# Two transformer layers on one core: ACT writes the rounded high parts from PSUM, and Pool splits the row minima

## The reference, cut to what matters

```
tgt1 = layer_norm(tgt, g1, be1)
score = einsum(q, k) / sqrt(HD) + (1 - mask) * -1e9      # q, k, v from tgt1
tgt = tgt + softmax(score) @ v @ Wo.T + bo
tgt = tgt + (memory @ Wg.T + bg)
tgt1 = layer_norm(tgt, g2, be2)
return tgt + relu(tgt1 @ W1.T + b1) @ W2.T + b2
```

## Time and profile before

| | |
|---|---|
| time, median of 3 runs | 1756.74 us (1756.67 to 1759.3) |
| profiled execution: its time | 1759.88 us |
| profiled execution: its span, first to last instruction | 1757.8 us |
| busy: PE, DVE, ACT, POOL | 1485.4, 1438.7, 939.3, 730.6 us |
| mean granted clock of PE | 0.939 |
| instructions | 42638 |

### The profile page before, as it was taken

The page is one execution under the profiler, slowest core; times in us unless marked ns, Lnnn a source line. Parts: engine busy times, 40 slices in busy tenths (PEclk is TensorE's granted clock), DMA queues, the critical chain, the costliest instruction groups (busy, mean ns, idle before and its releaser), DMA issues.

```text
span 1757.8 us, 42638 instructions
## 1 busy us (share of the span) xinstructions
PE 1485.4 (85%) x13376; PEld 1203.8 (68%) x13376; DVE 1438.7 (82%) x4560; ACT 939.3 (53%) x1849; POOL 730.6 (42%) x612
## 2 busy tenths in 40 slices
PE   2789999999999999677777777778889898998987
PEld 1568787888878887555655555556777776777756
DVE  2889888898988997787888788888888888888762
ACT  2666666666666654344444545454555545555451
POOL 3345444454544555423232222334444444444423
PEclk8799999999999999888898988899999999999998
DMA  5555445445544445454546464756444554445400
GB/s 139 135 120 130 106 96 114 103 108 118 116 114 96 121 96 129 104 120 96 120 103 116 100 117 107 138 114 118 99 95 92 113 112 92 93 100 112 88 25 12
DMA packets 163509, 185.73 MB, mean 106 GB/s; under 512 B 15952, under 2 KB 140240, under 8 KB 163408
## 3 DMA queue, kind: packets, MB, share of 16 engines
q1 hardware_dynamic: 163408, 184.57, 48.3%
HBM read 125.78 MB, written 58.72 MB: 105 GB/s over the span
## 4 chain that ended last, share of the span: by engine, by line
PE 55%; DVE 24%; issue 11%; POOL 3%; ACT 2%; DMA 2%; DVEq 1%; SPq 1%; ACTq 0%
PE d_ps L436 25%; PE d_ps L672 7%; PE o_ps L571 6%; DVE prob L849 6%; PE s_ps L493 6%; PE t_ps L507 4%; PE t_ps L541 4%; DVE top_rest L862 2%; PE m_ps L443 2%; POOL k_f L1062 2%; DMA k_stack<-parts 1%; DVE prob_t L1022 1%; DVE stats L871 1%; DVE o_q L911 1%; DVE k_part L934 1%
## 5 line engine op out<-in xcount | busy, mean ns | idle before, releaser
L720 ACT ACTIVATE prob_t<-t_ps 128x384 f32<-128x384 f32 (+1 forms) x512 | 275.7, 545 | 416.2 <-PE t_ps L541 212.6
L493 PE MATMUL s_ps<-k_stack,q_stack 96*128 96x256 bf16 (+1 forms) x1536 | 298.1, 277 | 102.5 <-DVE top L849 42.4
L711 ACT ACTIVATE prob<-prob,neg_max 128x256 f32<-128x256 f32 x512 | 233.0, 505 | 194.7 <-DVE neg_max L849 192.0
L493 PEld LDWEIGHTS s_ps<-k_stack,q_stack 96*128 96x128 bf16 x1536 | 116.2, 101 | 211.7 <-DVE top L849 66.0
L541 PE MATMUL t_ps<-q_stack,k_stack 108*128 108x256 bf16 (+1 forms) x1024 | 214.2, 276 | 8.7 <-ACT q_stack L728 8.6
L1062 POOL TENSOR_TENSOR h_lo<-h_f,h_hi 128x512 fp32r<-128x512 f32 x128 | 167.6, 1309 | 128.6 <-DVE h_hi L949 128.6
L849 DVE CUSTOM_DVE_ANT_0 prob<-s_ps,bias_sb 128x256 f32<-128x256 f32 x512 | 192.9, 416 | 22.0 <-PE s_ps L493 13.7
L571 PE MATMUL o_ps<-prob_t,v_sb 128*17 128x256 f32 (+1 forms) x3072 | 197.7, 377 | 0.0
L834 DVE TENSOR_REDUCE top<-s_ps 128x2 f32<-128x512 f32 x256 | 171.3, 680 | 23.0 <-PE s_ps L493 23.0
L728 ACT ACTIVATE q_stack<-o_ps 12x1024 bf16<-12x1024 f32 x128 | 130.2, 1017 | 106.7 <-PE o_ps L520 105.0
L849 DVE CUSTOM_DVE_ANT_0 prob<-s_ps,causal 128x128 f32<-128x128 f32 (+1 forms) x512 | 156.9, 349 | 34.6 <-PE s_ps L493 33.7
(11 more groups left out here) (113 smaller groups left out, 4148.3 us busy)
## 6 DMA issues: line engine op xcount, KB each, us to landing
q_stack<-parts SPq DMA_DIRECT2D x288, 128.0 KB, 4.1
k_stack<-parts SPq DMA_DIRECT2D x288, 128.0 KB, 6.4
parts<-q_part SPq DMA_DIRECT2D x96, 192.0 KB, 2.3
parts<-k_part SPq DMA_DIRECT2D x96, 192.0 KB, 2.3
ct_kept<-ct_hl SPq DMA_DIRECT2D x16, 512.0 KB, 7.7
x_in<-x_mid SPq DMA_DIRECT2D x32, 256.0 KB, 2.8
x_res<-x_mid SPq DMA_DIRECT2D x32, 256.0 KB, 2.9
ct_hl<-ct_kept SPq DMA_DIRECT2D x16, 512.0 KB, 8.0
```

Source lines behind the costliest of these rows:

```text
L493: last = mm(s_ps[:, h % 2, q * S:q * S + n], q_stack[0:ROWS, t.par, HEAD[h], q * P:(q + 1) * P], k_stack[0:ROWS, t.par, HEAD[h], 0:n], sta ...
L711: last = nc.scalar.activation(prob[:, h % 4, q, :], prob[:, h % 4, q, :], ACT.Exp, bias=neg_max[:, h % 4, q:q + 1], scale=-1.0)
L720: nc.scalar.activation(prob_t[:, h % 8, 0:n], t_ps[:, h % 2, 0:n], ACT.Exp, scale=-1.0)\
```

## The change

ACT now writes the high part out of PSUM too: each of its passes over a PSUM tile is made twice, first into the high part and then into the float32 tile, and one semaphore is raised after both. DVE's six kinds of rounding are gone, and what waited for them (`xt_h`, `x2t_h`, `ct_h`, `h_h`, `q_p1`, `k_p1`) waits for ACT's semaphore; the waits that guarded the high tiles against overwriting move from DVE to ACT. `top_split` moves from DVE to POOL, to the head of POOL's slots 4, 8, 12 and 0, with the tile of zeros. The top rows move one slot back on PE and ACT (R_LAG = 6 in place of CH + 1 = 5), and so do `E_LAG` (8) and the `PV_LAG` of passes 1 and 2 (12); `T_LAG` stays at 6. The normalisation of the attention's output, which stood in slots 9 and 10, stands at `NORM_AT` and the slot behind it: 6 and 7 in pass 0, 10 and 11 in passes 1 and 2. The diff, cut: the k tile goes as the q tile, and the roundings of q, k, ct and xt are removed from DVE as those shown.

```diff
@@ -64,9 +64,10 @@
...
-T_LAG, E_LAG = 6, 7
-PV_LAG = (8, 11, 11)
+R_LAG, T_LAG, E_LAG = 6, 7, 8
+PV_LAG = (8, 12, 12)
...
+NORM_AT = (6, 10, 10)
@@ -579,7 +580,7 @@
...
-        t, ht = head_at(st, h, CH + 1, KEYED)
+        t, ht = head_at(st, h, R_LAG, KEYED)
@@ -728,79 +729,89 @@
...
-    def affine(dst, col_g, col_b, done):
-        for k in range(KC):
-            last = nc.scalar.activation(dst[:, k, :], m_ps[:, k * S:(k + 1) * S], ACT.Identity,
-                                        bias=cols_sb[:, col_b + k:col_b + k + 1],
-                                        scale=cols_sb[:, col_g + k:col_g + k + 1])
+    def affine(high, dst, col_g, col_b, done):
+        for out_t in (high, dst):
+            for k in range(KC):
+                last = nc.scalar.activation(out_t[:, k, :], m_ps[:, k * S:(k + 1) * S], ACT.Identity,
+                                            bias=cols_sb[:, col_b + k:col_b + k + 1],
+                                            scale=cols_sb[:, col_g + k:col_g + k + 1])
...
-        t, ht = head_at(st, h, CH + 1, KEYED)
+        t, ht = head_at(st, h, R_LAG, KEYED)
...
             if has(st.old, (0,)):
-                act.wait_ge(ct_h.sem, ct_h.after(st.old))
...
-            affine(tf_b, c, c + 2, x2t_f)
+            affine(x2t_hi, tf_b, c, c + 2, x2t_f)
         if h == 3 and has(st.nxt):
...
-            if st.nxt.p == 0:
-                for m in range(KC):
-                    last = nc.scalar.activation(q_f[:, m, :], d_ps[:, 1, m * S:(m + 1) * S], ACT.Identity,
-                                                bias=cols_sb[:, C_BQ + m:C_BQ + m + 1], scale=-0.25)
-            else:
-                last = nc.scalar.activation(q_f[:, :, :], d_ps[:, 1, :].rearrange("p (m s) -> p m s", m=KC),
-                                            ACT.Copy, scale=-0.25)
+                act.wait_ge(q_written.of(st.cur), q_written.after(st.cur))
+            act.sem_inc(passed, 1)
+            for dst in (q_part[:, 0], q_f[:, :, :]):
+                if st.nxt.p == 0:
+                    for m in range(KC):
+                        last = nc.scalar.activation(dst[:, m, :], d_ps[:, 1, m * S:(m + 1) * S], ACT.Identity,
+                                                    bias=cols_sb[:, C_BQ + m:C_BQ + m + 1], scale=-0.25)
+                else:
+                    last = nc.scalar.activation(dst, d_ps[:, 1, :].rearrange("p (m s) -> p m s", m=KC),
+                                                ACT.Copy, scale=-0.25)
...
         if h == 5 and has(st.prev, (0,)):
...
-                act.wait_ge(x2t_h.sem, x2t_h.after(st.old))
...
-            nc.scalar.activation(tf_b[:, :, :], m_ps[:, :].rearrange("p (k s) -> p k s", k=KC), ACT.Copy)\
-                .then_inc(ct_f.sem, 1)
+                act.wait_ge(proj_mm.sem, proj_mm.after(st.old))
+                act.wait_ge(ct_stored.of(st.old), ct_stored.after(st.old))
+            turned = m_ps[:, :].rearrange("p (k s) -> p k s", k=KC)
+            act.sem_inc(passed, 1)
+            nc.scalar.activation(ct_hi[:, :, :], turned, ACT.Copy)
+            nc.scalar.activation(tf_b[:, :, :], turned, ACT.Copy).then_inc(ct_f.sem, 1)
         if 6 <= h <= 9 and has(st.old, MLP):
...
-                act.wait_ge(h_h.sem, h_h.after(st.old, n - 1))
...
-            for f in range(2):
-                c = C_B1 + FT * MLP.index(st.old.p) + 2 * n + f
-                last = nc.scalar.activation(h_f[:, n % 2, f, :], d_ps[:, n % 2, f * S:(f + 1) * S], ACT.Relu,
-                                            bias=cols_sb[:, c:c + 1])
+            for dst in (h_hi[:, 2 * n:2 * n + 2, :], h_f[:, n % 2]):
+                for f in range(2):
+                    c = C_B1 + FT * MLP.index(st.old.p) + 2 * n + f
+                    last = nc.scalar.activation(dst[:, f, :], d_ps[:, n % 2, f * S:(f + 1) * S], ACT.Relu,
+                                                bias=cols_sb[:, c:c + 1])
...
         if h == 14 and has(st.nxt2):
...
+                act.wait_ge(v_mm.sem, v_mm.after(st.nxt))
...
-            affine(tf_a, c, c + 2, xt_f)
+            affine(xt_hi, tf_a, c, c + 2, xt_f)
         t, ht = head_at(st, h, LAG, (0,))
@@ -850,22 +859,6 @@
...
-    def top_split(st, t, c):
-        dve.wait_ge(u_done.sem, u_done.after(t, CH * (c + 1)))
...
     def statistics(src, st_t, done):
@@ -909,45 +899,23 @@
...
-        if h == 10 and has(st.prev):
+        if has(st.prev) and h == NORM_AT[st.prev.p] + 1:
...
-        if h == 3 and has(st.old, MLP):
-            dve.wait_ge(x2t_f.sem, x2t_f.after(st.old))
-            v.tensor_copy(x2t_hi[:, :, :], tf_b[:, :, :]).then_inc(x2t_h.sem, 1)
         if h == 3 and has(st.nxt, (0,)):
...
-        if 7 <= h <= 10 and has(st.old, MLP):
-            n = h - 7
-            dve.wait_ge(h_done.sem, h_done.after(st.old, n + 1))
-            v.tensor_copy(h_hi[:, 2 * n:2 * n + 2, :], h_f[:, n % 2]).then_inc(h_h.sem, 1)
-        if h == 10 and has(st.prev):
+        if has(st.prev) and h == NORM_AT[st.prev.p] + 1:
@@ -1064,18 +1029,37 @@
...
+    def top_split(st, t, c):
+        pool.wait_ge(u_done.sem, u_done.after(t, CH * (c + 1)))
+        before, cb = (t, c - 2) if c >= 2 else (st.prev if t is st.cur else st.old, c + 2)
+        if has(before, KEYED):
+            pool.wait_ge(top_mm.sem, top_mm.after(before, cb + 1))
+        src, part = top[:, c % 2], top_part[:, c % 2]
+        g.tensor_tensor(part[:, :, :, 0], src, zeros[:, :, :], ALU.add).then_inc(top_1.sem, 1)
+        pool.wait_ge(top_1.sem, top_1.after(t, c + 1))
+        g.tensor_tensor(top_rest[:, :, :], src, part[:, :, :, 0], ALU.subtract).then_inc(top_r.sem, 1)
+        pool.wait_ge(top_r.sem, top_r.after(t, c + 1))
+        g.tensor_tensor(part[:, :, :, 1], top_rest[:, :, :], zeros[:, :, :], ALU.add).then_inc(top_2.sem, 1)
+        pool.wait_ge(top_2.sem, top_2.after(t, c + 1))
+        g.tensor_tensor(part[:, :, :, 2], top_rest[:, :, :], part[:, :, :, 1], ALU.subtract)\
+            .then_inc(top_3.sem, 1)
     def slot(st, h):
+        t, ht = head_at(st, h, CH, KEYED)
+        if t and ht % CH == 0:
+            top_split(st, t, ht // CH)
         if h == 15 and has(st.nxt2):
-            pool.wait_ge(xt_h.sem, xt_h.after(st.nxt2))
+            pool.wait_ge(xt_f.sem, xt_f.after(st.nxt2))
...
         if h == 3 and has(st.old, MLP):
-            pool.wait_ge(x2t_h.sem, x2t_h.after(st.old))
+            pool.wait_ge(x2t_f.sem, x2t_f.after(st.old))
...
         if h == 4 and has(st.nxt):
-            pool.wait_ge(q_p1.sem, q_p1.after(st.nxt))
+            pool.wait_ge(q_done.sem, q_done.after(st.nxt))
...
         if h == 5 and has(st.nxt):
-            pool.wait_ge(k_p1.sem, k_p1.after(st.nxt))
+            pool.wait_ge(k_done.sem, k_done.after(st.nxt))
...
```

More of the change, by code:

```diff
@@ L1022, in slot @@
                     v.tensor_copy(prob_t[:, ht % 8], t_ps[:, 1, :]).then_inc(pt_odd.sem, 1)
-                if h == 15 and has(st.nxt2):
-                    dve.wait_ge(xt_f.sem, xt_f.after(st.nxt2))
-                    if st.nxt:
-                        dve.wait_ge(v_mm.sem, v_mm.after(st.nxt))
-                    v.tensor_copy(xt_hi[:, :, :], tf_a[:, :, :]).then_inc(xt_h.sem, 1)
                 if st.s is not None:
@@ L1089, in slot @@
                     n = h - 7
-                    pool.wait_ge(h_h.sem, h_h.after(st.old, n + 1))
+                    pool.wait_ge(h_done.sem, h_done.after(st.old, n + 1))
                     sub(h_lo[:, 2 * n:2 * n + 2, :], h_f[:, n % 2], h_hi[:, 2 * n:2 * n + 2, :], h_l.sem)
```

69 lines of the change are left out of this document (21 added, 48 removed).

## The result

The changed kernel takes 1729.63 us (median of 4 runs, 1723.13 to 1733.37) against 1756.7 for the kernel before beside it (4 runs, 1751.75 to 1759.3): ratio 0.9845, 95% interval [0.9808, 0.9883]. The forecast was 1699. It is faster, by 27 us where 58 were forecast. The profiled execution took 1728.53 us with a span of 1726.7, 31 less than that of before.

What follows compares the result with a forecast made beforehand. Three limits: PE nearly full in pass 0, nothing full in pass 1, PE at 90% with waits in pass 2. Terms +28 - 51 - 35 = -58 us took the median 1756.7 to 1699 us; eight-in-ten range 1655 to 1750.

Steps and rivals of the forecast that it cites:

- its DMA chain into the stacks has slack now: Pass 1: q up to 1.4 us later is harmless, PE having waited for k_stack 3 times in 13 steps, 3.0 us.
- The wait for o_q: Pass 1, PE ahead of the top rows' small matmul: 2.6 of 3.0 us a step go.
- The wait for the row minima: Pass 1, PE ahead of the scores: half of the 2.6 us a step goes, 1.3.
- The clock: Pass 1: slow clock costs PE 2.5 us a step; with less waiting a third, 0.8, returns.
- The bare copy: Pass 1, slot 6: no product covers ACT's copy of the top rows before the keyed scores, +1.3 us a step.
- Pass 0: ACT's second passes lengthen its chain to the V product; net +2.0 us a step, 14 steps, +28 us.
- Pass 2: Wait behind o_q shrinks by 1.8, clock returns 0.7, h_f's 1.6 stays; -2.5 us a step, 14 steps, -35 us.
- The split on POOL: Four dependent 128x8 operations on POOL: 1.2 to 3.2 us a chunk, taken as 1.4, hidden in two slots of pass 1.
- C: Pass 1 meets another limit: POOL's 3.2 us a chunk makes stacks late, or the copy costs fully; 1730, chance 0.2.
- A: PE's clock falls in pass 0 as PE waits in the W1 slots; slower, 1776 us, chance 0.08.
- B: ACT bounds pass 0 whole, +5.7 us a step, +80 us, the rest as forecast; 1751 us, chance 0.12.
- D: Both slack ends better: pass 1 reaches its PE time, -5 a step, pass 2 -4; 1654 us, chance 0.15.

Runs made afterwards that it cites:

- short stacks: Changed kernel, but in pass 1 the last three of six copies each of q and k into the stacks move 2 of 8 heads: 1702.11 us, ratio 0.9688.
- the two versions with short stacks: Shortened pass-1 copies into the stacks, on the changed kernel (1702.11 us) and on it with all six roundings back on DVE (1665.26 us).
- the split alone: Changed kernel with all six kinds of rounding back on DVE, the row-minima split staying on POOL: 1694.56 us, ratio 0.9635.

## Why the prediction missed

**The step that failed** is in what POOL takes: "its DMA chain into the stacks has slack now". The sum for pass 1 put this chain at nothing. It had about 1 us of slack at the old step and none at the forecast one, and it cost 1.84 us a step: short stacks take 1729.63 - 1702.11 = 27.5 us off the time, nearly the 30.6 that the forecast missed by. In a step of the kernel before ACT began k_f at 943.65, the last copy of k was issued by 957.22, and PE's wait for the stacks ended at 966.28: 22.6 us in all. That is one of the steps that waited; over 11 steps the time from the start of k_f to the last landing is 18.5 to 22.5, median 20.6. ACT takes k in slot 4 and the scores want it in slot 0 of the next step, three quarters of a step later: 21.8 us at 29.05 a step and 19.3 at the forecast 25.7. So the trace of before held the answer. Few waits (3.0 us in 13 steps) showed that the stacks mostly came in time at 29 us, and not by how much. The change even shortened the way, since POOL's first subtraction of k started 1.2 us after ACT's first pass over k (948.85 - 947.69) where it was 2.8 before (946.42 - 943.65); in the step shown it took 968.04 - 947.69 = 20.4 us, and 19.0 in the median. That the stacks set the step is shown by the two versions with short stacks (-1.8 and -2.4 us a step).

**Pass 1, term by term.** The wait for o_q gave 3.0 for 2.6. The wait for the row minima was to give 1.3 and gave 0.3 (28.2/11.9 = 2.4 after, 2.6 before). The clock gave (1 - 0.93) x 253/11.9 = 1.5 for 2.5 before, so 1.0 for 0.8. The bare copy, +1.3, was a misreading: the sections ahead of the prediction and the prediction say that `T_LAG` stays 6, but the diff shows 7, and the copy keeps its slot between. Its wait is 0.47 a step before and after; where it was made bare, it took 0.7 of wait and no time in pass 1. The stacks cost 2.1 - 0.2 = 1.9. Sum: -3.0 - 0.3 - 1.0 + 1.9 = -2.4; -2.16 was measured. Errors partly hid each other: 1.3 charged for a copy that isn't bare stood against 1.9 left out for the stacks and 1.0 too much for the row minima. Without the misread term the forecast would have been -4.7 a step.

**Pass 0** was right in its size: +2.0 forecast, +1.78 measured. The chain over ACT came out at 18.7 us for 19.2. PE waits 28.7/12.2 = 2.3 us a step for ACT and has got back 0.8 of its 1.7 us of waits for DVE, where nearly all was forecast. Where it waits was half right: V for the last h_f, yes, but the larger wait is W1's first product behind k, which the prediction had not seen, and in the step shown W1's third doesn't wait.

**Pass 2** has the right mechanism and too large a size: -1.79 for -2.5. The wait for o_q went whole (2.1 for 1.8), the clock gave 1.0 for 0.7, h_f 1.15 a step where 1.6 was to stay. Unforeseen are 0.76 behind k_f and 0.73 behind prob_t, both on ACT's queue and both absent with the split alone, whose step is 33.47. So the term mis-sized here is what ACT's second passes cost in pass 2: the sum had them only as a wait for h_f that stays, and the split alone shows 34.66 - 33.47 = 1.2 us a step.

**The split on POOL** was priced at 1.4 us a chunk. In pass 1 it takes 1.1 (four operations of 0.21 to 0.23, 0.28 to 0.38 from start to start), and nothing holds it here, other than in the version with the roundings on DVE:

```profile
L1039 POOL TENSOR_TENSOR top_part<-top,zeros 128x8 bf16<-128x8 f32 x48 | 11.1, 232 | 68.5 <-DVE top L858 68.5
L1041 POOL TENSOR_TENSOR top_rest<-top,top_part 128x8 f32<-128x8 f32 x48 | 10.0, 209 | 3.8
```

**The rivals.** The time came out where C had put it, 1730, with pass 1 short of its forecast and the stacks late. That is luck in part: C had pass 1 at -20 us and pass 2 at -35, measured are -32 and -25, and neither of C's two causes is at work. POOL needs nothing like 3.2 us a chunk, and the copy isn't bare; made bare, it costs nothing in pass 1. A did not happen (clock 0.99 in pass 0), nor B, nor D, which had passed over the stacks.

**Left open:** why the same twelve copies land later in some versions or executions than in others, and a step of pass 1 takes 26.9 to 28.6 us with them; why k's second pass is free in pass 0 where q's with it is not; and what the later slots bring without the split on POOL.

## What to carry to other kernels

When a step is to get shorter, list the chains of fixed length that run beside it (computed, split, written, loaded again) and set each against the slots it has in the shorter step: here a transfer that was waited for 3 times in 13 steps was a bound 1 us away, and not slack. Read from the chain whose part it is that leads: here k was in the stack last, and q's third part held it up. Judge a change of two halves by each half alone; here one half gave 61 us and the other took 35 of them, which the sum of the two hid. Work moved onto an engine whose queue is already in step with PE can cost time even if that engine's busy share is 53 to 65%; how much depends on its place in the queue (x2t's pass all of its 0.9 us in pass 0, h's four 0.8 of 2.8, k's by itself nothing).
